# Half of the softmax scaling of an attention stage moved from VectorE to ScalarE

## The reference

```python
def _L0_attn_ref(x, w_qkv, w_proj):
    qkv = (x @ w_qkv.T).reshape(B, N, 3, H, hd)          # H = 16, hd = 128
    q, k, v = (qkv[:, :, 0], qkv[:, :, 1], qkv[:, :, 2])
    att = jnp.einsum('bnid,bnjd->bnij', q, k) * scale
    att = jax.nn.softmax(att, axis=-1)
    out = jnp.einsum('bnij,bnjd->bnid', att, v)
    out = out.transpose(0, 2, 1, 3).reshape(B, N, D)
    return out @ w_proj.T
...
x = x + _L0_attn_ref(_layernorm(x), L0_attn_w_qkv, L0_attn_w_proj)
x = x + _L0_ffn_ref(_layernorm(x), L0_ffn_kernel, L0_ffn_bias)
```

## Time and profile before

| | us |
|---|---|
| time, median of 2 runs | 907.75 (905.78 to 909.73) |
| the profiled execution | 907.14 |
| its span, slowest core (core 6) | 905.6 |
| spans of all cores | 894.7 to 905.6 |
| busy in the span: PE, DVE, ACT, POOL | 690.0, 565.5, 323.4, 111.2 |
| mean granted clock of PE | 0.866 |

### The profile page before, as it was taken

How to read it: one execution, slowest core, us unless ns; L and a number is a source line. 1 busy time by engine, 2 the same in 40 slices (tenths; PEclk the granted TensorE clock), 3 DMA queues, 4 the chain that set the end, 5 groups by cost and what they waited for, 6 DMA issues and landing times.

```text
span 905.6 us, 11027 instructions; the slowest of 8 cores (894.7 to 905.6 us)
## 1 busy us (share of the span) xinstructions
PE 690.0 (76%) x3584; PEld 339.7 (38%) x3584; DVE 565.5 (62%) x949; ACT 323.4 (36%) x363; POOL 111.2 (12%) x93
## 2 busy tenths in 40 slices
PE   0147899999999999994565559964967547979790
PEld 0123344444444444443444424520433223434340
DVE  3343345455555544436777729981788895999996
ACT  3376343344334334435555521210221324433320
POOL 1001111111112111100000000012000000123214
PEclk9998999999999999996555569975897967989996
DMA  9451979999999999746632254379322200111112
GB/s 165 120 180 38 86 71 146 148 162 149 149 154 148 157 150 103 72 45 165 174 46 36 39 173 138 117 157 176 86 71 70 94 0 1 47 47 47 77 63 93
DMA packets 116984, 94.20 MB, mean 104 GB/s; under 512 B 101184, under 2 KB 101312, under 8 KB 113856
## 3 DMA queue, kind: packets, MB, share of 16 engines
q0 software_dynamic: 103680, 33.56, 37.2%
q1 hardware_dynamic: 13248, 59.94, 19.5%
HBM read 118.65 MB, written 8.39 MB: 140 GB/s over the span
## 4 chain that ended last, share of the span: by engine, by line
DVE 23%; PE 13%; issue 9%; DMA 5%; ACT 3%; DVEq 1%; POOLq 0%; POOL 0%; ACTq 0%; SPq 0%
DMA wpb<-wpT 4%; PE pF L501 3%; PE pF L504 3%; DVE bnbuf L590 2%; DVE cols L655 2%; DVE ttile L798 2%; PE pF L537 2%; DVE cols L801 2%; ACT Ebuf L357 1%; ACT aTTbuf L365 1%; PE pF L343 1%; DVE ktb L687 1%; DMA ktb<-wkT 1%; DVE xr L556 1%; DVE kti L691 1%
## 5 line engine op out<-in xcount | busy, mean ns | idle before, releaser
L286 PE MATMUL pF<-aT,wqb 128*128 128x512 bf16 x736 | 278.9, 379 | 3.1 <-DMA wqb<-wqkvT 3.1
L288 PE MATMUL pF<-aT,wqb 128*128 128x512 bf16 x736 | 278.9, 379 | 0.0
L501 PE MATMUL pF<-wpb,sT 128*128 128x512 bf16 x256 | 105.9, 414 | 24.4 <-DMA wpb<-wpT 22.3
L537 PE MATMUL pF<-qk,xqs 128*128 128x512 bf16 x512 | 118.8, 395 | 3.7 <-ACT xqs L884 3.7
L504 PE MATMUL pF<-wpb,sT 128*128 128x512 bf16 x256 | 106.2, 415 | 0.0
L286 PEld LDWEIGHTS pF<-aT,wqb 128*128 128x128 bf16 x736 | 72.0, 98 | 90.6 <-issue 4.0
L288 PEld LDWEIGHTS pF<-aT,wqb 128*128 128x128 bf16 x736 | 72.0, 98 | 86.6
L301 POOL DMA_DIRECT2D wqb<-wqkvT x48 | 55.1, 1147 | 334.9 <-PE pF L288 245.1
L113 DVE CAST qT<-pF 128x512 bf16<-128x512 f32 x16 | 42.6, 2664 | 66.6 <-PE pF L288 53.2
L113 DVE CAST vT<-pF 128x512 bf16<-128x512 f32 x16 | 42.9, 2680 | 58.5 <-PE pF L288 58.5
L537 PEld LDWEIGHTS pF<-qk,xqs 128*128 128x128 bf16 x512 | 51.7, 102 | 67.6 <-issue 13.1
(11 more groups left out here) (116 smaller groups left out, 844.0 us busy)
## 6 DMA issues: line engine op xcount, KB each, us to landing
wqb<-wqkvT POOLq DMA_DIRECT2D x48, 512.0 KB, 9.3
ktc<-wkT SPq DMA_DIRECT2D x32, 512.0 KB, 7.7
ktb<-wkT SPq DMA_DIRECT2D x32, 512.0 KB, 3.9
xbuf<-x_att SPq DMA_DIRECT2D x8, 1024.0 KB, 7.1
xr<-x_res SPq DMA_DIRECT2D x8, 1024.0 KB, 9.5
wpb<-wpT POOLq DMA_DIRECT2D x32, 256.0 KB, 6.0
out<-xr SPq DMA_DIRECT2D x7, 1024.0 KB, 3.8
bias_b<-bias SPq DMA_DIRECT2D x1, 1024.0 KB, 4.8
```

The source lines that it names most:

```text
L286: tn.matmul(pa[:, :], wch, aT[:, 1024 * c:1024 * c + 512], start=st, stop=sp)
L288: mm = tn.matmul(pb[:, :], wch, aT[:, 1024 * c + 512:1024 * c + 1024], start=st, stop=sp)
L501: tn.matmul(pF[2 * (idx % 2)][:, :], lhs, wpb[:, 1024 * m:1024 * m + 512], start=st, stop=sp)
L537: mm = tn.matmul(pF[u][:, :], xqs[Mt % 2][:, 128 * c:128 * (c + 1)], qk[:, 2048 * c + 512 * u:2048 * c + 512 * (u + 1)], start=(c == 0), s ...
```

## The change

Blocks 0 and 1 of each group are still scaled by DVE. Blocks 2 and 3 are now scaled by ACT, by two activations of the function Copy with the reciprocal as a per-partition scale. They stand in ACT's program between Exp(g) and T(g-1). The reciprocal signals a semaphore of its own, cRcp, for which ACT waits. ACT signals cAsS after its second block, and PE waits for it as well as for cAsc before the transposes of Abuf.

```diff
@@ tensor
                 if k >= 0:
                     tn.wait_ge(S_("cAsc"), k + 1)
+                    tn.wait_ge(S_("cAsS"), k + 1)
@@ scalar
                     inc(s.activation(Ebuf[g % 2][:, :], pF[g % 2][:, :], AF.Exp,
                                      bias=col(80), scale=SCALE), "cExp")
 
+                if g < NG:
+                    s.wait_ge(S_("cRcp"), g + 1)
+                    if g >= 2:
+                        s.wait_ge(S_("cAtT"), g - 1)
+                    for j in range(2, 4):
+                        instr = s.activation(Abuf[g % 2][:, 128 * j:128 * (j + 1)],
+                                             Embuf[g % 2][:, 128 * j:128 * (j + 1)],
+                                             AF.Copy,
+                                             scale=C_R4(g % 2)[:, j:j + 1])
+                        if j < 3:
+                            inc(instr, "selfS")
+                    inc(instr, "cAsS")
                 k = g - 1
@@ vector
-                    h_rc = inc(v.reciprocal(C_R4(p), C_S4(p)), "selfV")
+                    h_rc = inc(v.reciprocal(C_R4(p), C_S4(p)), "cRcp")
                     if g >= 2:
                         v.wait_ge(S_("cAtT"), g - 1)
                     wt(v, h_rc)
-                    for j in range(4):
+                    for j in range(2):
...
-                        if j < 3:
+                        if j < 1:
                             inc(instr, "selfV")
                     inc(instr, "cAsc")
```

## The result

The changed kernel takes 976.5 us (median of 11 runs), where the kernel before takes 908.2 (10 runs). The ratio is 1.0748, with a 95% interval of 1.0724 to 1.0772: 68 us slower. Runs in which the cores of a die took some per cent longer at a lower granted clock count in these medians, but in no ratio of this document. The forecast was 974. The profiled execution of the changed kernel took 971.44 us, and its slowest core is now core 4, with a span of 969.9 us.

What follows compares the result with a forecast made beforehand. The prediction took two equal rings of waits, 3.37 us a group, to bound the attention stage. One merged ring adds 29 x 2.20 = 63.9 us, start 2.07, end 1.04: 907.14 + 67.0 = 974.1 us, range 965 to 986.

Steps and rivals of the forecast that it cites:

- The ring: Attention stage, Exp through reciprocal, two ACT copies, aTTbuf copy and scores to next Exp: 5.57 us a group, 3.37 before.
- The step of a copy: On ACT, each added 128x128 copy moves the next instruction by 0.30 us, estimated between 0.20 and 0.61.
- Start and end: Attention stage's edges: +2.07 us up to Exp(2), +1.04 us from Exp(31) to the last copy to sT.
- Nothing given back: After the attention stage: all of the added time, +67.0 us, is passed on to the kernel's time.
- Hidden: Rival: the copies fill ACT's idle time in the attention stage and DVE's lighter load gains 5.3 us: 902 us, chance 0.02.
- only the copies' time: Rival: the aTTbuf copy comes late only by two copies' work on ACT, 19 us in all: 926 us, chance 0.02.
- ACT reloads its tables: Rival: Exp and scaled copy need different tables, two loads per group on ACT, 82 us more: 1056 us, chance 0.02.
- Part given back: Rival: the later ktb wait shrinks; halved, 5 us return (969); more than 10 us, about 955, chance 0.03.
- Explanation P: Loss through PE's added wait for ACT's half of Abuf; the prediction held those copies long done by then.

Runs made afterwards that it cites:

- wait_only: Kernel before, plus only ACT's wait for the reciprocal of group g between Exp(g) and the copy to aTTbuf of g-1; no ACT copies: ratio 1.0583.
- ahead: Kernel before, reordered without the split: PE does vT transpose and scores two groups ahead, ACT's Exp follows the aTTbuf copy: ratio 0.9778.
- deep_split: Kernel before, reordered with scores three groups ahead and four V8buf buffers, plus the change's split, ACT's two scalings ahead of the aTTbuf copy: ratio 0.9666.
- deep: Kernel before, reordered without the split: PE does vT transpose and scores three groups ahead, V8buf has four buffers: ratio 0.9757.

## Why the prediction was right

Step by step, in its own terms:

- **The ring.** 2.29 + 0.15 + 0.60 + 2.53 = 5.57 us was forecast; the timeline of the changed kernel has 2.28 from Exp to the end of the reciprocal, 0.15 to ACT, 0.60 for the two copies and 2.51 from T to the next Exp, 5.54 us. The mean over the 29 groups from Exp(2) to Exp(31) is (582.88 - 420.84) / 29 = 5.59, since in 4 of the 30 groups from 420 us on ACT idles 2.03 to 2.10 us for the reciprocal instead of 1.75. The delay of 0.28 to 0.35 us falls each time at another hand-over (ahead of DVE's reciprocal at 462.0, of ACT's first copy at 501.4, of DVE's sum at 517.3, of its mask at 572.6). What it is stays open; it makes 1.3 us.
- **The step of a copy**, the one term without a row, was taken as 0.30 us between 0.20 and 0.61. The copies take 394 ns on average and start 0.30 us apart. The estimate from the Trainium skill's page "ScalarE: Activation LUTs" (What ACT_TABLE_LOAD costs), 386 ns and a step of 0.29 us, agrees too.
- **Start and end.** From Exp(0) to Exp(2) 8.61 us was forecast and 8.35 measured; from Exp(31) to the last copy to sT 6.78 and 6.74.
- **Nothing given back.** What follows the stage takes 379.7 us after 380.4.
- **The rivals.** "Hidden" and "only the copies' time" fall by wait_only, where no copy exists and 50 us are lost. "ACT reloads its tables" falls by the trace: one load in the stage, as before. "Part given back" falls by the windows. Explanation P of the experiments, which the prediction had ruled out in a sentence, falls by the wait of PE for ACT's half of Abuf: 3.7 us in the whole stage, all in the first group.

That the place in the queue is the cause is shown from both sides: the wait alone makes most of the loss, and the same instructions behind the other two copies lose only 10 us. The prediction said nothing of how the split would do at a better place. The experiments add that it loses there too in the order of this kernel, by 1.1%, and gains about 1% (0.9666 against 0.9757) only in an order where DVE sets the pace and ACT's wait holds nothing back; in ahead the first held and the second did not, and the split lost there.

The stage grew by 67.2 us in the slowest cores (forecast 67.0), and the times by 68. The two profiled executions differ by less, 64.3 us: in the changed one the first Exp came 2.0 us earlier, at 412.49 instead of 414.47, where the forecast had held it fixed, and what follows the start of the last copy to sT was 0.9 us shorter. The start of the stage lies between 411.0 and 418.6 us in the ten traces, so the 2.0 us can't be put down to the change.

## What to carry to other kernels

Before moving work to an idle engine, ask what stands behind it in that engine's queue. An engine with half of its time idle can be in the middle of the ring that sets the pace, and a wait placed ahead of the step that starts the next round costs the full overlap, here 1.6 us a group for no work at all. Move work off an engine once that engine is the one without gaps, and only to a place in the other queue where the wait for it holds nothing of the next round back. Here that took an order with the scores three groups ahead, and then the same split gained; with two groups ahead, where DVE had almost no gaps either, it still lost.

## What the runs showed of the hardware that was not expected

In deep_split alone was the granted clock of PE over its lower level in the body of the stage; in the other kernels it is 0.50 there. The window of 420 to 460 us, first of deep_split, then of deep:

```profile
420.00:460.00 40.00, 26.07 (x268) 21.88 (x268) 34.18 (x108) 37.51 (x86) 4.58 (x9) 0.71 0.81 198
```

```profile
420.00:460.00 40.00, 31.43 (x251) 24.34 (x252) 35.19 (x123) 25.24 (x46) 4.24 (x8) 0.50 0.73 182
```

At 0.71 on average, deep_split had the upper level of 2.4 GHz for part of the time; deep stayed at the lower. Three shorter windows of deep_split, around one rise and one fall:

```profile
467.10:473.70 6.60, 5.29 (x48) 4.84 (x48) 5.76 (x18) 6.42 (x15) 0.53 (x1) 0.50 0.47 74
473.90:477.10 3.20, 1.67 (x23) 1.24 (x22) 2.76 (x8) 3.02 (x8) 0.53 (x1) 1.00 0.49 63
477.30:480.60 3.30, 2.81 (x27) 2.42 (x24) 2.91 (x10) 3.28 (x9) 0.53 (x1) 0.50 0.28 47
```

Four transposes of Abuf take 0.63 us at 472.52, ahead of the rise, and 0.38 at 474.69, after it. Ahead of the rise PE worked from 469.71 to 471.58, stood idle for 0.56 us, and worked again from 472.14 on. Ahead of the fall it stood idle for 0.33 us until 474.31 and for 1.19 us until 476.71. In deep it stood idle for 0.41 and 0.15 us in each group and stayed at the lower level. What decided was not tried. The time of the stage hardly depends on it, since DVE sets the pace: its sums start at 469.33, 471.59, 473.85, 476.11 and 478.37, 2.26 us apart at either level.

The step from the copy of V8 to the mask on DVE is 0.33 us, though the copy lasts 0.42: here neighbours on DVE overlap by 0.08 to 0.09 us when the second doesn't need the first. I had counted 0.45, which is why deep came out at 2.58 us a group in its timeline, and not at 2.7.
